# A new fixed order for the last four feed-forward tiles, and the last row statistics by head group

## What is computed

```python
def _reorder_quantize_x(x, idx):
    scale = jnp.max(jnp.abs(x)) / GLOBAL_DIV
    xr = (x / scale)[:, idx]
    scale_x = jnp.max(jnp.abs(xr), axis=1, keepdims=True) / FP8_MAX
    return _fp8(xr / scale_x), scale_x, scale
...
x = x + tanh(g_xattn[0]) * mha(layernorm(x), ctx, ctx)        # ctx: 4 x 1601 x 512, causal
h = layernorm(x)
qx, sx, sc = _reorder_quantize_x(h, up_idx)
g = _qlinear(qx, sx, sc, w_gate, up_idx, out_idx=down_idx)
u = _qlinear(qx, sx, sc, w_up, up_idx, out_idx=down_idx)
t = silu(g) * u
qt, st, sct = _reorder_quantize_x(t, down_idx)
x = x + tanh(g_ffn[0]) * _qlinear(qt, st, sct, w_down, down_idx)
```

## Time and profile before

| what | before |
|---|---|
| median of 3 runs | 1157.04 us (1155.66 to 1158.47) |
| the profiled execution, its own time | 1155.15 us |
| its span | 1153.4 us, mean granted TensorE clock 0.952 |
| busy in the span | TensorE 969.0 us (84%), VectorE 862.0 (75%), ScalarE 656.3 (57%), GpSimd 312.9 (27%) |
| the last of these 40 slices (28.8 us each) | TensorE 3, 4, 4, 4 tenths; VectorE 6, 7, 7, 5 tenths |

### The profile page before, as it was taken

One profiled execution on the slowest core, in us unless ns is written; L12 is line 12 of the kernel. 1 busy time (PEld: TensorE's weight loads), 2 busy tenths in 40 slices (PEclk: granted clock), 3 DMA queues, 4 the chain that ended last, 5 costly groups with the idle time before them and its releaser, 6 DMA issues.

```text
span 1153.4 us, 21093 instructions
## 1 busy us (share of the span) xinstructions
PE 969.0 (84%) x7770; PEld 399.7 (35%) x7770; DVE 862.0 (75%) x1450; ACT 656.3 (57%) x1343; POOL 312.9 (27%) x338
## 2 busy tenths in 40 slices
PE   4588889888879989999889999999889999983444
PEld 2233333333323333333334333333334343442222
DVE  7768789887747887777687878787778777436775
ACT  2165567676636666666556666666566666763322
POOL 3012334332101423232322232232323232433212
PEclk9998899999989999999999999999899999995766
DMA  7942423231572212124822221108621020000000
GB/s 149 159 118 67 117 67 94 66 78 35 103 98 53 71 47 49 44 53 71 125 46 63 67 55 41 48 24 128 81 56 40 20 48 11 2 10 10 10 10 19
DMA packets 155119, 70.69 MB, mean 61 GB/s; under 512 B 111032, under 2 KB 142856, under 8 KB 155016
## 3 DMA queue, kind: packets, MB, share of 16 engines
q1 hardware_dynamic: 153256, 63.57, 26.8%
q0 software_dynamic: 1760, 5.77, 1.8%
HBM read 39.08 MB, written 4.19 MB: 38 GB/s over the span
## 4 chain that ended last, share of the span: by engine, by line
PE 42%; DVE 38%; issue 11%; ACT 4%; POOL 3%; DMA 1%; SPq 0%; POOLq 0%; DVEq 0%; ACTq 0%
DVE mch L1066 18%; PE ps L863 12%; PE ps L839 8%; PE ps L884 6%; PE ps L777 5%; PE ps L907 3%; DVE ff L982 2%; DVE ff L978 2%; DVE ff L986 2%; PE ps L782 2%; ACT pr L629 1%; DVE upd L1109 1%; DMA qst<-mrow 1%; DVE cmb L1099 1%; PE ps L845 1%
## 5 line engine op out<-in xcount | busy, mean ns | idle before, releaser
L629 ACT ACTIVATE pr<-ps 128x512 f32<-128x512 f32 (+4 forms) x832 | 397.1, 530 | 247.0 <-PE ps L839 125.8
L1066 DVE TENSOR_REDUCE mch<-ps 128x2 f32<-128x1024 f32 (+4 forms) x416 | 432.0, 1055 | 68.2 <-PE ps L777 32.8
L863 PE MATMUL ps<-pr,vf 128*33 128x512 f32 (+4 forms) x1664 | 379.8, 536 | 0.0
L839 PE MATMUL ps<-qst,kst 97*64 97x512 f16 (+4 forms) x1600 | 250.6, 371 | 17.7 <-DMA qst<-mrow 11.2
L777 PE MATMUL ps<-kTh,qTh 32*128 32x512 f16 (+4 forms) x832 | 156.0, 373 | 60.0 <-DVE mch L1066 40.9
L777 PEld LDWEIGHTS ps<-kTh,qTh 32*128 32x128 f16 x832 | 39.5, 91 | 277.9 <-DVE mch L1066 106.9
L839 PEld LDWEIGHTS ps<-qst,kst 97*64 97x64 f16 (+1 forms) x1600 | 77.3, 111 | 107.3 <-ACT pr L629 57.1
L863 PEld LDWEIGHTS ps<-pr,vf 128*33 128x33 f32 (+1 forms) x1664 | 86.9, 113 | 57.1 <-issue 5.5
L1142 DVE SCALAR_TENSOR_TENSOR ff<-ps,scs,wsb 128x352 f32<-128x352 f32 x56 | 32.6, 583 | 71.3 <-PE ps L884 71.2
L884 PE MATMUL ps<-wgu,t_T 128*64 128x352 bf16 x768 | 66.5, 316 | 0.0
L445 POOL TENSOR_TENSOR t_q<-ff 128x768 bf16<-128x768 f32 (+1 forms) x24 | 40.4, 1682 | 87.5 <-DVE ff L986 87.5
(11 more groups left out here) (152 smaller groups left out, 1188.1 us busy)
## 6 DMA issues: line engine op xcount, KB each, us to landing
kst<-kTh SPq DMA_DIRECT2D x128, 100.1 KB, 2.2
ksrc<-in_ctx SPq DMA_DIRECT2D x16, 768.0 KB
vf<-in_ctx SPq DMA_DIRECT2D x48, 256.0 KB, 5.1
kst<-kTl SPq DMA_DIRECT2D x64, 100.1 KB, 2.2
xs<-in_x SPq DMA_DIRECT2D x16, 256.0 KB, 4.1
qst<-qTh SPq DMA_DIRECT2D x128, 32.0 KB, 1.9
...
```

The source lines that it names most:

```text
L629: nc.scalar.activation(pr[0:kn, n % NP, q0:S], ps[0:kn, j, q0:S], ACT.Exp, scale=SCALE).then_inc(ex_done, 1)
L839: last = nc.tensor.matmul(ps[a:e, j, q0:S], kst[s][0:ST, r, k0 + a:k0 + e], qst[s][0:ST, r, q0:S], start=True, stop=(t < DT))
L863: nc.tensor.matmul(ps[64 * j:64 * j + VW, 2 + pp % 2, q0:S], vf[0:kn, t, h, :], pr[0:kn, n % NP, q0:S], start=(t == 0), stop=(t == NT - 1) ...
L1066: nc.vector.tensor_reduce(mch[:, qt, 2 * hp:2 * hp + 2, c], both[:, :, 0:k1 - k0], AX.X, ALU.max).then_inc(dve_free, 1)
```

## The change

```diff
-    ROWS_AT, UP_AT, HIDDEN_AT, DOWN_AT = 5, (7, 9, 11, 13), 23, 25
+    NORM_ROWS, ROWS_STATS, SCALE_ROWS, ROUND_ROWS, SUB_ROWS, TURN_ROWS = (0, 90), (1, 93), (2, 94), (3, 95), (4,), (5, 96)
+    UP, TAKE_UP = (7, 9, 11, 13, 97, 99, 104, 107), (7, 9, 11, 13)
+    GATE, BEND, GATE_UP = (7, 9, 11, 13, 100, 101, 106, 108), (8, 10, 12, 14, 101, 103, 107, 109), (8, 10, 12, 14, 102, 104, 108, 110)
+    HIDDEN, HIDDEN_STATS, SCALE_HIDDEN = (10, 12, 14, 16, 104, 105, 110, 112), (16, 113), (17, 18, 114, 116)
+    ROUND_HIDDEN, SUB_HIDDEN, TURN_HIDDEN, KEEP_HIDDEN = (18, 19, 116, 117), (20, 21), (23, 117), (23, 119)
+    DOWN, OUT = (25, 120), (25, 125)
...
+    def tail_base(n):
+
+        return LAST + 17 + 14 * (n - TAIL) - 100
...
+        steady = [(n, at - tile_base(n)) for n in range(TAIL)]
+        tail = [(n, at - tail_base(n)) for n in range(TAIL - 1, TILES)]
+        return ([(n, k) for n, k in steady if 0 <= k < TILE_STEPS and (n < TAIL - 1 or k <= 16)]
+                + [(n, k) for n, k in tail if 90 <= k < 127 and (n >= TAIL or k >= 114)])
...
+        def last_stats(dve, s, g, qt):
+            b = B - 1
+            dve.wait_ge(xs_done, (b * NG + g + 1) * PAIRS)
+            s.step(nc.vector.bn_stats(part[:, qt, g, :], xs[:, b % 3, qt, g * P:(g + 1) * P]))
+
+        def last_variance(dve, s):
+            s.settle()
+            dve.nop(nofuse=True)
+            for qt in range(QT):
+                s.step(nc.vector.bn_aggr(mvf[:, qt, :], part[:, qt, :, :].rearrange("p g n -> p (g n)")))
+            s.settle()
+            nc.vector.tensor_scalar(ve[:, :], mvf[:, :, 1], EPS, None, ALU.add).then_inc(varf_ready, 1)
...
-            if n >= TAIL:
+            if n >= TAIL - 1:
                 dve.wait_ge(qt_added, 2 * n + half_of + 1)
...
+                if GALL - NG < gg < GALL and u in OUT_STATS_AT:
+                    last_stats(dve, s, gg % NG - 1, OUT_STATS_AT.index(u))
                 if at == LAST + 6:
                     for qt in range(QT):
-                        out_stats(dve, s, B - 1, qt)
-                    out_variance(dve, s, B - 1)
+                        last_stats(dve, s, NG - 1, qt)
+                    last_variance(dve, s)
...
-    nc = bacc.Bacc("TRN2", target_bir_lowering=False, num_devices=1)
+    nc = bacc.Bacc("TRN2", target_bir_lowering=False, num_devices=1, dynamic_dma_scratch_size=8192)
```

More of the change, by code:

```diff
@@ L82, in tile_base @@
     def tile_base(n):
[L84 to L92, removed]
+        return STEPS * (n + NG) + 15
+    def tail_base(n):
+        return LAST + 17 + 14 * (n - TAIL) - 100
+    END = tail_base(TILES - 1) + 127
     def tiles_at(at):
-        return ([(n, at - tile_base(n)) for n in range(TILES) if ROWS_AT < at - tile_base(n) < TILE_STEPS]
-                + [(n, at - rows_base(n)) for n in range(TILES) if 0 <= at - rows_base(n) <= ROWS_AT])
+        steady = [(n, at - tile_base(n)) for n in range(TAIL)]
+        tail = [(n, at - tail_base(n)) for n in range(TAIL - 1, TILES)]
+        return ([(n, k) for n, k in steady if 0 <= k < TILE_STEPS and (n < TAIL - 1 or k <= 16)]
+                + [(n, k) for n, k in tail if 90 <= k < 127 and (n >= TAIL or k >= 114)])
     def before_in_set(n):
@@ L116, in flamingo_gated_block, with in_tail @@
     banks, before_in_bank, latest, dve_count, act_count = {}, {}, {}, {}, {}
+    def in_tail(job):
+        return job[0] in ("rows", "up", "hidden", "down") and job[1] >= TAIL - (job[0] in ("hidden", "down"))
     def numbered(*job):
-        if job[0] in ("rows", "up", "hidden", "down") and job[1] >= TAIL:
-            banks[job] = 2 * (sum(1 for other in banks if other[0] in ("rows", "up", "hidden", "down") and other[1] >= TAIL) % 4)
+        if in_tail(job):
+            banks[job] = 2 * (sum(1 for other in banks if in_tail(other)) % 4)
         else:
@@ L151, in flamingo_gated_block @@
         for n, k in tiles_at(at):
[L152 removed]
+            if k in TURN_ROWS:
                 numbered("rows", n)
[L154 to L156 removed]
+            if k in UP:
+                numbered("up", n, UP.index(k) % GC)
+            if k in TURN_HIDDEN:
                 numbered("hidden", n)
[L158 removed]
+            if k in DOWN:
                 numbered("down", n)
@@ L204, in flamingo_gated_block @@
         stat = sb("stat", [P, QT, 6])
+        part = sb("part", [P, QT, NG, 6])
         mv, mvf = sb("mv", [P, QT, 2]), sb("mvf", [P, QT, 2])
@@ L537, in _ @@
                 for n, k in tiles_at(at):
-                    if k == 4 and n < TAIL:
+                    if k in SUB_ROWS:
                         round_rows(pool, n)
[L540 to L544, removed]
+                    if k in GATE_UP:
+                        gate_up(pool, n, GATE_UP.index(k) % GC)
+                    if k in SUB_HIDDEN:
+                        round_hidden(pool, n, SUB_HIDDEN.index(k))
+                    if k in OUT:
                         add_hidden(pool, n)
@@ L713, in _ @@
                 for n, k in tiles_at(at):
-                    if k == 0:
+                    if k in NORM_ROWS:
                         norm_rows(act, n)
-                    if k == 2:
+                    if k in SCALE_ROWS:
                         scale_rows(act, n)
-                    if k == ROWS_AT:
+                    if k in TURN_ROWS:
                         turn_rows(act, n)
-                    if k in UP_AT and n < TAIL:
-                        take_up(act, n, UP_AT.index(k))
-                    if k - 1 in UP_AT:
-                        bend_gate(act, n, UP_AT.index(k - 1))
-                    if k in (17, 18):
-                        scale_hidden(act, n, k - 17)
-                    if k == HIDDEN_AT:
+                    if k in TAKE_UP:
+                        take_up(act, n, TAKE_UP.index(k))
+                    if k in BEND:
+                        bend_gate(act, n, BEND.index(k) % GC)
+                    if k in SCALE_HIDDEN:
+                        scale_hidden(act, n, SCALE_HIDDEN.index(k) % 2)
+                    if k in KEEP_HIDDEN:
                         turn_hidden(act, n)
```

32 lines of the change are left out of this document (17 added, 15 removed).

## The result

| what | before | changed |
|---|---|---|
| median of the runs | 1157.36 us (4 runs, 1155.66 to 1158.47) | 1167.24 us (4 runs, 1165.80 to 1170.33) |
| ratio | | 1.0089, 95% interval 1.0066 to 1.0111 |
| the profiled execution, its span, mean granted clock | 1155.15, 1153.4, 0.952 | 1165.88, 1164.1, 0.945 |

What follows compares the result with a forecast made beforehand. No engine is full in the tail, a chain jumping between VectorE and TensorE. Tail end 1163.0 plus 1.9 for statistics gave 1164.9 against a span of 1153.4, + 11.5 on the median 1157.04: 1168.5 us, range 1160 to 1176.

Steps and rivals of the forecast that it cites:

- The order gives nothing back: Tail tiles: the new order's chain sums to 22.45 us a tile, no better than 22.5 and 23.1 before.
- H12: End of hstats of tile 12 on VectorE; sign: near 1079 us, prediction wrong if below 1075.
- The new waits: VectorE in the tail: idle before gate1 on U1, near 1.2 us, and before gate3 on U3, 2 to 3 us.
- part 1: Chain of one tail tile in the new order: 22.45 us, with U2 slow at 2.5 and D at 3.2.
- Part 2: VectorE's hround and rround stand still while GpSimd's gup runs: 7 x 0.93 = 6.5 us, bounds 0 and 10.2.
- the stalls cost nothing: Rival for hround and rround: GpSimd waits for VectorE instead, all else as forecast; 1162.0 us, chance 0.15.
- wrong if no L982 exceeds 0.6 us: Sign in hround on VectorE: L978, L982 or L986 near 1.5 us where a gup runs, else the prediction is wrong.
- The statistics: Last batch's statistics: opening path 1.4 us shorter, new VectorE work of 1.0 us in each of groups 13, 14 and 15.
- The term of groups 13 and 14: Early statistics beside attention: these two groups nearly fully paid, group 15 free; 1.9 us, bounds 0 and 2.9.
- The rival on the other side: Tail: VectorE becomes the bound, clock stays at 2.4 GHz, no stalls; a tile costs 19.0, total 1148.8 us; chance 0.08.
- No change: Rival in the tail: no stalls, D and U1 fast each time; 1156.4 us, chance 0.07.
- slower still: Rival in the tail: clock rises late, D 4.5, U3 and U1 2.5, + 3.3 a tile; 1182 us, chance 0.05.

Runs made afterwards that it cites:

- e2: Changed kernel with the old statistics of the last batch, so the new order only; ratio 1.0094 to the kernel before.
- e5: Changed kernel with hround of a tile moved ahead of the next tile's gate1 on VectorE; ratio 1.0034 to the kernel before.
- e4: Changed kernel with U3 of a tile put ahead of D of the tile before on TensorE; ratio 0.9984 to the kernel before.
- e9: Changed kernel with many idle matmuls that nobody reads where TensorE would rest in the tail; ratio 0.9976 to the kernel before.
- e3: Changed kernel with GpSimd's product gup cut from 352 to 32 columns in chunks 1 and 3; ratio 1.0029 to the kernel before.

## Why the prediction was right, point by point

- **The order gives nothing back, and the loss is in the opening and the last tile.** Right. Predicted were a period of 24.35, a last tile of 21.1 and 16.2 to the end; measured 23.89, 21.04 and 16.4. From hstats.11 to H12 the working gives 1077.0 - 1041.14 = 35.9 (its steps add up to 1077.15); measured 35.8. e2 shows that this part alone makes 1.0094. Start to start, the measure of the working, the chain of tile 13's period closes:

| step | predicted | measured |
|---|---|---|
| rowsT and rcopy | 1.2 | 1.15 |
| U0 and U1 to gate1 | 4.3 | 4.10 |
| gate1 | 0.6 | 0.51 |
| hround with its stall | 6.73 | 6.44 |
| second half of hidT | 0.7 | 0.64 |
| U2 | 2.5 | 2.35 |
| D | 3.2 | 3.71 |
| U3 to gate3 | 1.2 | 1.40 |
| gate3 and rround with its stall | 3.88 | 3.59 |
| period | 24.3 | 23.89 |

- **The new waits.** Right in place. Gate1' waits on U1' for 0.93 us with hround queued behind it, and e5 shows what this costs: about 5 of the 6.7 us by which its tail is shorter. Gate3' waits on U3', 3.22 against "2 to 3", and e4 shows that this is the largest of them. That U0' runs slow behind a rest was in the working. Not foreseen was that this rest hangs on the same queue (U3' behind D): with U3' first, e4's U0 and U1 take 2.58.
- **The terms of TensorE.** U2 2.56 by its row against 2.5. U0 with U1 4.07 against 4.3. D 3.87 by its row and 3.71 start to start against 3.2, mis-sized by 0.5: more of D was slow than the bit over 1 us that part 1 counted. The split is not fixed by the order: in e2, D.12 took 2.64 and U0 with U1 4.91, at nearly the same period (23.69). e9 confirms the mechanism for all four: with the rests filled they take 1.39, 2.58 and 2.54.
- **The stalls.** The mechanism and the count of seven were right, the size was not. Part 2 took the whole gup, 0.93, for each, 6.5 us in all; measured were 0.60 each, 4.2 in all. The rows at hand showed less than a whole GpSimd instruction too: 1.97 for 0.49 is 1.48 lost beside an L445 of 1.98, and 1.24 for 0.52 is 0.72. The rival "the stalls cost nothing" falls with e3. This error of -2.3 us, D's of +0.5 in each of four tiles (+2.0) and small ones of both signs nearly cancel. That is why the total came so close, and it is luck.
- **The signs.** One of them fails by its letter: "wrong if no L982 exceeds 0.6 us". L993, which is L982 there, took at most 0.56 in hround and rround of the changed kernel. The stall sits in L997 (L986 of before), which the sum did not tell apart. Its 1.56 matches the "near 1.5" only because the stall was shorter than priced; with 0.93 it would have been 1.89. H12 "near 1079" came out at 1079.06, with 0.94 us from the statistics and 1.2 of scatter where 1.9 were priced: luck as well.
- **The statistics.** The opening gained 1.35 against 1.4: four statistics took 0.85 instead of 1.0, and the aggregate grew by 0.25 instead of 0.07. The term of groups 13 and 14 was mis-sized, 0.94 measured against 1.9; that group 15 is free was right. What the halved descriptor scratch costs ahead of H8 isn't separated from the scatter there.
- **The rival on the other side** (the clock stays at 2.4 GHz) was priced at 19.0 a period without stalls. e9 is that case with its stalls: 20.48, and 0.6 x 3 = 1.8 above 19.0 would be 20.8. It fell in the changed kernel, whose clock was 0.72 over a period, and it came true once the rests were filled. "No change" fell with the interval (1.0066 and up), and "slower still" with U3 at 1.36 and D at 3.87, not 2.5 and 4.5.
